# Fourteen batches' gate exponentials on ScalarE, later selections of diagonals, and a y ring of ten places

## The chip, the cores and the metric

The kernel runs on one core of a Trainium2 chip. The core has TensorE (matrix products into PSUM), VectorE, ScalarE and GpSimd (elementwise work, each with its own strengths), SyncE (here it issues transfers only), and 16 DMA engines that all queues share. The engines run their own instruction streams and wait for each other by semaphores. The metric is the device time of one execution in microseconds (us).

## What is computed

One block of a network on 16 batches of 256 tokens with 128 features, in float32: an attention-like part, then a mixture of 8 experts of which each token takes the best two. The second part, cut to what matters here:

```python
router_logits = (xhat * router_ln_w + router_ln_b) @ router_w + router_b
routing_weights, selected = jax.lax.top_k(router_logits, 2)
routing_weights = jax.nn.softmax(routing_weights, axis=-1)
h = gelu(xn_e @ w1[e] + b1[e])            # for each expert e of the token
eo = h @ w2[e] + b2[e]
combined = sum_k routing_weights[k] * eo[selected[k]]
y = _ln_stats(combined) * out_ln_w + out_ln_b
x = x + gb * y
```

With two logits a token's weights are p/(1+p) and 1/(1+p), where p = exp(second logit - first logit). These p are the gates' exponentials.

## The kernel before

The attention part runs over the 16 batches as a software pipeline of 21 iterations (`pipeline(iteration)`), each engine with its own `iteration`. Tokens are kept as 32 tiles of 128 (two a batch). During the pipeline the routing is worked out in groups of two batches (`choose`, `place`): `top` holds each token's best logits, `slot` the row of each token's copy in the DRAM buffer `xe_dram`, where rows are sorted by expert. GpSimd writes the rows there by indirect DMA (`scatter`). The last group, batches 14 and 15, comes through only after the expert tiles have begun.

The expert part then runs over 71 tiles of 128 sorted rows, `n` from 0 to 70. For one tile:

- SyncE loads the rows into one of 6 places `xg` (L322). At tile 16 it also issues the 2 MB load of `outf` (L325), the output factors.
- TensorE transposes (`turn`, L1611), multiplies by w1 (`up`, L1620, eight matmuls) and by w2 (`down`, L1630, eight matmuls). In one round it does the transpose of tile j, the up of j-2 and the down of j-3.
- VectorE, in `prepare(n)`, computes the destination rows `idxr` (L1198), scales the transposed tile (L1202) and copies the expert's w1 (L1205); then in `finish(n-3)` it adds the bias to the product and writes `y` (L1240). Between tiles 14 and 19 `prepare` also carries the table of the late tiles (`late_counts` to `late_rows`, L976 to L1001). At every even tile from 30 to 60 it adds a factor to x (L1232).
- ScalarE computes the Gelu (`hidden`, L734).
- GpSimd stores the tile's 128 rows of `y` to DRAM by indirect DMA (`store`, L482).

The places of `y` and `idxr` are a ring (`RING`, `scat`) of eight: `prepare(n)` and `finish(n)` wait until the store of tile n-8 has landed (`need_ring`). Each place has its own semaphore, `scat0` to `scat7`.

The gates: at tile 20 VectorE subtracts the two logits for all 32 token tiles (L1221, `pw`, 128x32). After the store of tile 18 GpSimd raises e to them (L487, a power on 128x32). At tile 26 VectorE makes the two weights of each token (L1224 to L1226, `gates`). From tile 28 on, at every fifth tile, GpSimd turns the weights of four token tiles into diagonal matrices (L492, `diag`, 128x1024), eight times (`DIAGONALS`).

At the end (`NG` = 8 groups of four token tiles) SyncE loads the y rows back in token order, TensorE multiplies them by the diagonals and sums (L1765), VectorE and ScalarE normalize, and the results are stored.

The order of the instructions on each engine is written out by hand; nothing schedules it.

Of the kernel before, what the change touches and what calls it, by code (L numbers as in the profile page):

```python
# [10 lines left out]
ACT = mybir.ActivationFunctionType  # L11
ALU = mybir.AluOpType
# [34 lines left out]
def build(nc, inp, out):  # L47
# [7 lines left out]
    with ExitStack() as ctx:  # L55
# [5 lines left out]
        def sem(name):  # L61
# [98 lines left out]
        LAG_U, LAG_D, LAG_S = 2, 3, 5  # L160
        RING = dict(gath=6, scat=8)
        LOADS = ((0,), (1, 2), (3, 4, 5), (6, 7))
        POOLED = NG - 2
        PARTS = [(g, 0, GROUP) for g in range(NG - 1)] + [(NG - 1, 0, 2), (NG - 1, 2, 2)]
        DIAGONALS = range(28, 28 + 5 * NG, 5)
        FACTORS = range(30, 30 + 2 * NB, 2)
# [23 lines left out]
            oT_mm sq_rdy ms_mm rsln_rdy rs_rdy t1_rdy on_rdy wob_rdy out_mm x1_rdy mv2_rdy rs2ln_rdy ve2_rdy rs2_rdy xn2_rdy xn2T_tp h2T_rdy h3_mm h3_rdy sq3_rdy rs3ln_rdy ve3_rdy rs3_rdy xrow_rdy  # L190
            set_route pad_fill pad_st endrow_rdy bt_rdy oh_rdy rank_mm slot_rdy xs_early xs_late table_rdy rb_mm rb_rdy dve_chain
            f_ld f_st f_halves f_s0 f_s pw_rdy f_fin outb_rdy
            idxr_rdy gath0 gath1 gath2 gath3 gath4 gath5 tile_tp xgT_rdy w1c_rdy up_mm hid_rdy down_mm y_rdy
            scat0 scat1 scat2 scat3 scat4 scat5 scat6 scat7
            yk_ld0 yk_ld1 yk_ld2 yk_ld3 diag_rdy acc_mm st4_rdy mv4_rdy rs4ln_rdy rs4_rdy nmr_rdy yn_rdy yo_rdy out_pool out_rdy out_st""".split()
# [60 lines left out]
        def need_tile(eng, name, j):  # L256

            if 0 <= j < NS:
                eng.wait_ge(S[name], j + 1)
# [91 lines left out]
        def _(pool):  # L351
# [48 lines left out]

            nc.gpsimd.memset(euler[:], float(np.e)).then_inc(S["f_halves"], 1)

# [73 lines left out]
            def store(n):  # L476
# [7 lines left out]
                if n == 18:  # L484
                    pool.wait_ge(S["f_halves"], 1)
                    pool.wait_ge(S["f_s0"], 1)
                    nc.gpsimd.tensor_tensor(pw[:, :, 1], euler[:], pw[:, :, 0], ALU.pow).then_inc(S["f_s"], 1)  # L487
                if n in DIAGONALS:
# [83 lines left out]
        def _(act):  # L572
# [154 lines left out]
            def hidden(n):  # L727

                if not 0 <= n < NS:
                    return  # L730
                need_tile(act, "down_mm", n - 2)
                need_tile(act, "up_mm", n)
                for c in range(NC):
                    last = nc.scalar.activation(hid[:, n % 2, c, :], up_bank[n % 2][:, c * P:(c + 1) * P], ACT.Gelu,  # L734
                                                bias=w1c[:, n % 3, FF + c:FF + c + 1])
                last.then_inc(S["hid_rdy"], 1)
                if 20 <= n < 20 + NE and n % 2 == 1:
                    put_pad(act, n - 20)
# [98 lines left out]
        def _(dve):  # L837
# [165 lines left out]
            def constants():  # L1003
# [7 lines left out]
                nc.vector.tensor_copy(bt_sb[:, :, LNW - FF], vecT[:, R_LNW:R_LNW + NE])  # L1011
                nc.vector.tensor_copy(bt_sb[:, :, LNB - FF], vecT[:, R_LNB:R_LNB + NE]).then_inc(S["bt_rdy"], 1)

# [170 lines left out]
            def prepare(n):  # L1184
# [3 lines left out]
                if n == 0:  # L1188
# [3 lines left out]
                    link(nc.vector.tensor_copy(w1s[:, :, FF:FF + NC], bt_sb[:, :, 0:NC]))  # L1192
                    chosen[n] = expert(n)
                e = chosen[n]
                need_ring(dve, "scat", n - RING["scat"])
# [24 lines left out]
                if n == 20:  # L1220
                    tt(pw[:, :, 0], top[:, :, 1], top[:, :, 0], ALU.subtract).then_inc(S["f_s0"], 1)  # L1221
                if n == 26:
                    dve.wait_ge(S["f_s"], 1)
                    link(ts(gates[:, :, 0], pw[:, :, 1], 1.0, None, ALU.add))  # L1224
# [574 lines left out]
```

## Time and profile before

| | us |
|---|---|
| median of 3 runs | 505.92 |
| lowest and highest | 505.23, 505.97 |
| the profiled execution | 503.87 |
| its span, first to last instruction | 502.1 |
| busy: TensorE (matmuls) | 438.9 |
| busy: VectorE | 397.6 |
| busy: GpSimd | 353.1 |
| busy: ScalarE | 317.2 |

The span is shorter than the execution by 1.8 us, which lie around it. The busy times are sums over stages with different limits, so no one of them tells what a step is worth: for that one has to go to the stage and see which wait ends last there. A row of the timeline reads: start, length, engine, line, operation, what it writes and reads, and in brackets the time that the engine sat idle before it and what released it. "PE" is TensorE, "PEld" its loading of weights, "DVE" VectorE, "ACT" ScalarE, "POOL" GpSimd, "SP" SyncE, a "q" behind it the engine's queue. All buffers of the expert part are parts of one tensor `work`, so `xgT`, `w1c`, `hid`, `xg` and `y` all appear as `work`; lines tell them apart.

### The profile page before, as it was taken

Reading aid. Unit: us, or ns where it says so; the run is one execution under the profiler, and the core shown is the slowest. Engines: PE = TensorE matmul, PEld = TensorE weight load, DVE = VectorE, ACT = ScalarE, POOL = GpSimd, SP = SyncE. Lnnn points to the kernel's source line nnn. Section 1 sums busy time; section 2 is a strip of 40 time slices with the busy share of each in tenths; the row PEclk is TensorE's granted clock in tenths of the full one; section 3 lists DMA queues with packets and bytes.
Section 4 is the critical chain, followed back from the end, with each engine's and each line's share of the span. In section 5 each row is a group of like instructions: output and inputs, shape, how many; then the busy total and the mean of one; then the engine's idle time right before and its main releaser. Section 6 shows DMA issues by size and latency. Waiting matters only on the chain.

```text
span 502.1 us, 11499 instructions
## 1 busy us (share of the span) xinstructions
PE 438.9 (87%) x3266; PEld 363.8 (72%) x3266; DVE 397.6 (79%) x1133; ACT 317.2 (63%) x812; POOL 353.1 (70%) x404
## 2 busy tenths in 40 slices
PE   3589999999899899889799666899789999999990
PEld 1366777776677677667667444799689999999990
DVE  2579998999989979999999965566665788776485
ACT  1166788888578578688679634675345555555575
POOL 4675875689889889899887526276468876666532
PEclk9999999999889889899999667599989999999996
DMA  6950000000000000000000141227233322226344
GB/s 157 238 148 1 7 8 7 1 17 19 25 17 22 21 23 19 21 26 13 24 23 20 47 150 34 62 70 245 64 90 80 83 86 73 69 74 212 131 134 125
DMA packets 33933, 33.66 MB, mean 67 GB/s; under 512 B 7036, under 2 KB 27680, under 8 KB 33744
## 3 DMA queue, kind: packets, MB, share of 16 engines
q1 hardware_dynamic: 27600, 22.39, 16.3%
q0 software_dynamic: 4320, 9.22, 5.5%
q10 hardware_dynamic: 1952, 1.32, 1.0%
q8 instruction: 29, 0.48, 0.4%
q14 instruction: 32, 0.26, 0.2%
HBM read 20.43 MB, written 12.48 MB: 66 GB/s over the span
## 4 chain that ended last, share of the span: by engine, by line
PE 45%; DVE 21%; POOL 19%; issue 6%; ACT 4%; DMA 2%; DVEq 1%; ACTq 1%; POOLq 0%
PE sa_ps L1620 11%; POOL xe_dram L387 6%; PE bank L1630 5%; PE sa_ps L1630 5%; PE sa_ps L1398 4%; POOL lgs L421 2%; POOL A_sb L394 2%; PE bank L1537 2%; DVE z L1046 2%; PE bank L1611 2%; PE bank L1470 2%; POOL xn L472 2%; DMA y_dram<-work,idxr 2%; PE bank L1471 2%; PE bank L1553 2%
## 5 line engine op out<-in xcount | busy, mean ns | idle before, releaser
L734 ACT ACTIVATE work<-sa_ps,work 128x128 f32<-128x128 f32 x284 | 81.2, 369 | 68.7 <-PE sa_ps L1620 68.7
L482 POOL DMA_INDIRECT y_dram<-work,idxr x71 | 72.5, 1021 | 45.4 <-DVE idxr L1198 32.0
L387 POOL DMA_INDIRECT xe_dram<-xrow,slot x64 | 72.8, 1137 | 24.1 <-issue 13.7
L1620 PE MATMUL sa_ps<-work 128*128 128x128 f32 x568 | 80.0, 285 | 0.4
L1620 PEld LDWEIGHTS sa_ps<-work 128*128 128x128 f32 x568 | 71.3, 197 | 1.4 <-issue 0.7
L1398 PE MATMUL sa_ps<-Px,wvT 64*128 64x128 f32 (+1 forms) x288 | 41.9, 341 | 3.8 <-DVE Px L1102 3.7
L1398 PEld LDWEIGHTS sa_ps<-Px,wvT 64*128 64x128 f32 x288 | 34.2, 194 | 13.8 <-DVE Px L1102 9.2
L421 POOL TENSOR_TENSOR lgs<-lgs,rsum 128x256 f32<-128x256 f32 x32 | 30.6, 974 | 16.9 <-DVE rsum L1062 16.9
L1630 PE MATMUL bank<-w2s,work 128*128 x280 | 38.2, 281 | 3.5 <-DVE work L1240 3.5
L1630 PE MATMUL sa_ps<-w2s,work 128*128 x288 | 39.0, 279 | 1.2 <-DVE work L1240 0.8
L394 POOL TENSOR_SCALAR_AFFINE_SELECT A_sb<-A_sb 128x768 f32<-128x768 f32 (+1 forms) x32 | 19.9, 647 | 26.3 <-ACT A_sb L705 26.1
L1630 PEld LDWEIGHTS bank<-w2s,work 128*128 128x128 f32 x280 | 34.8, 195 | 4.1 <-issue 4.1
L1630 PEld LDWEIGHTS sa_ps<-w2s,work 128*128 128x128 f32 x288 | 35.7, 195 | 1.8 <-issue 1.7
L1553 PE MATMUL bank<-lT,low 128*128 128x256 f32 x128 | 31.9, 392 | 0.6 <-ACT lT L693 0.6
L472 POOL TENSOR_SCALAR xn<-x_sb,mv,rs 128x128 f32<-128x128 f32 x32 | 31.8, 997 | 0.4 <-POOL rs L429 0.4
L705 ACT COPY A_sb<-sa_ps 128x1536 f32<-128x1536 f32 x16 | 23.0, 1440 | 13.2 <-PE sa_ps L1398 13.2
L1391 PE MATMUL sa_ps<-qT,kT 32*128 32x128 f32 (+1 forms) x288 | 30.9, 333 | 0.2
L1202 DVE TENSOR_SCALAR work<-bank,bt_sb 128x128 f32<-128x128 f32 x71 | 29.0, 408 | 2.4 <-issue 0.4
L1205 DVE COPY work<-work 128x516 f32 x71 | 30.7, 433 | 0.1
L1391 PEld LDWEIGHTS sa_ps<-qT,kT 32*128 32x128 f32 x288 | 24.0, 189 | 6.7 <-issue 5.6
L1198 DVE SCALAR_TENSOR_TENSOR idxr<-work,bt_sb 128x1 uint32<-128x1 f32 x71 | 21.2, 298 | 9.4 <-DMA y_dram<-work,idxr 7.7
L1553 PEld LDWEIGHTS bank<-lT,low 128*128 128x128 f32 x128 | 23.0, 189 | 5.3 <-issue 0.9
(278 smaller groups left out, 1127.7 us busy)
## 6 DMA issues: line engine op xcount, KB each, us to landing
work<-xe_dram SPq DMA_DIRECT2D x71, 69.5 KB
work<-in_w SPq DMA_DIRECT2D x1, 2048.0 KB, 9.6
outf<-outf_dram SPq DMA_DIRECT2D x1, 2048.0 KB
xrow<-y_dram SPq DMA_DIRECT2D x4, 512.0 KB, 6.2
out<-x_sb SPq DMA_DIRECT2D x7, 256.0 KB, 2.4
y_dram<-work,idxr POOLq DMA_INDIRECT x71
modb<-mod_dram SPq DMA_DIRECT2D x16, 64.0 KB, 2.8
xe_dram<-xrow,slot POOLq DMA_INDIRECT x64, 2.4
```

What stands on the lines that cost most here:

```text
L387: nc.gpsimd.indirect_dma_start(xe_dram, bass.IndirectOffsetOnAxis(slot[:, 4 * batch + column:4 * batch + column + 1], 0), xrow[:, tile, :] ...
L394: last = nc.gpsimd.affine_select(out=blocks, in_=blocks, compare_op=ALU.is_ge, fill=0.0, base=0, pattern=[[0, n] for n in blocks.shape[1:- ...
L421: last = nc.gpsimd.tensor_tensor(p, p, rsum[:, b % 2, tile * H:(tile + 1) * H].unsqueeze(2).broadcast_to([P, H, M]), ALU.mult)
L472: last = nc.gpsimd.tensor_scalar(xn[:, b % 2, tile, :], x_sb[:, 2 * b + tile, :], mv1[:, b % 4, tile, 0:1], rs1[:, b % 4, tile:tile + 1], ...
L482: nc.gpsimd.indirect_dma_start(y_dram, bass.IndirectOffsetOnAxis(idxr[:, n % RING["scat"]:n % RING["scat"] + 1], 0), y[:, n % RING["scat"] ...
L734: last = nc.scalar.activation(hid[:, n % 2, c, :], up_bank[n % 2][:, c * P:(c + 1) * P], ACT.Gelu, bias=w1c[:, n % 3, FF + c:FF + c + 1])
L1205: nc.vector.tensor_copy(w1c[:, n % 3], w1s[:, bass.ds(e, 1), :].squeeze(1)).then_inc(S["w1c_rdy"], 1)
L1391: return mm(o, kT[d, b % 2, s * P:(s + 1) * P], qT[d, b % 2, t], start=True, stop=True)
L1398: return mm(o, wvT[m, b % 4, h // 2, s * P:(s + 1) * P], Px[m, b % 2, h // 2, t], start=True, stop=True)
L1553: last = mm((b4, b5)[n // 2][:, (n % 2) * T:(n % 2 + 1) * T], low2[:, n, :], lT[:, b % 2, :], start=True, stop=True)
L1620: last = mm(up_bank[n % 2][:, c * P:(c + 1) * P], w1c[:, n % 3, c * P:(c + 1) * P], xgT[:, n % 3, :], start=True, stop=True)
L1630: last = mm(down_bank[n % 2][:, 0:D], hid[:, n % 2, c, :], w2s[:, bass.ds(chosen[n], 1), c, :].squeeze(1), start=c == 0, stop=c == NC - 1)
```

## The change

The ring of y rows and index rows gets ten places instead of eight, with two more semaphores. The subtraction is done in two parts: token tiles 0 to 27 (batches 0 to 13, `AHEAD` = 28) at the start of tile 0, the last four at tile 20 as before. ScalarE computes the exponentials of the first 28 with its Exp before its first Gelu; GpSimd's power is left with the last 4. The diagonals are made at tiles 36, 40, ... 64 instead of 28, 33, ... 63. The semaphore `f_halves` is replaced by a third count of `set_route`, and an increment that nobody waited for (`bt_rdy`) is gone.

```diff
@@
-        RING = dict(gath=6, scat=8)
+        RING = dict(gath=6, scat=10)
...
-        DIAGONALS = range(28, 28 + 5 * NG, 5)
+        DIAGONALS = range(36, 36 + 4 * NG, 4)
+        AHEAD = 2 * (NB - 2)
@@ GpSimd
-            nc.gpsimd.memset(euler[:], float(np.e)).then_inc(S["f_halves"], 1)
+            nc.gpsimd.memset(euler[:], float(np.e)).then_inc(S["set_route"], 1)
...
                 if n == 18:
-                    pool.wait_ge(S["f_halves"], 1)
-                    pool.wait_ge(S["f_s0"], 1)
-                    nc.gpsimd.tensor_tensor(pw[:, :, 1], euler[:], pw[:, :, 0], ALU.pow).then_inc(S["f_s"], 1)
+                    pool.wait_ge(S["set_route"], 3)
+                    pool.wait_ge(S["f_s0"], 2)
+                    nc.gpsimd.tensor_tensor(pw[:, AHEAD:NT, 1], euler[:, AHEAD:NT], pw[:, AHEAD:NT, 0], ALU.pow).then_inc(S["f_s"], 1)
@@ ScalarE, hidden(n)
+                if n == 0:
+                    act.wait_ge(S["f_s0"], 1)
+                    nc.scalar.activation(pw[:, 0:AHEAD, 1], pw[:, 0:AHEAD, 0], ACT.Exp).then_inc(S["f_s"], 1)
                 need_tile(act, "down_mm", n - 2)
@@ VectorE, constants()
-                nc.vector.tensor_copy(bt_sb[:, :, LNB - FF], vecT[:, R_LNB:R_LNB + NE]).then_inc(S["bt_rdy"], 1)
+                nc.vector.tensor_copy(bt_sb[:, :, LNB - FF], vecT[:, R_LNB:R_LNB + NE])
@@ VectorE, prepare(n), n == 0
                     chosen[n] = expert(n)
+                    tt(pw[:, 0:AHEAD, 0], top[:, 0:AHEAD, 1], top[:, 0:AHEAD, 0], ALU.subtract).then_inc(S["f_s0"], 1)
@@ VectorE, prepare(n)
                 if n == 20:
-                    tt(pw[:, :, 0], top[:, :, 1], top[:, :, 0], ALU.subtract).then_inc(S["f_s0"], 1)
+                    tt(pw[:, AHEAD:NT, 0], top[:, AHEAD:NT, 1], top[:, AHEAD:NT, 0], ALU.subtract).then_inc(S["f_s0"], 1)
                 if n == 26:
-                    dve.wait_ge(S["f_s"], 1)
+                    dve.wait_ge(S["f_s"], 2)
```

How it stands on the engines, in rows that give line, operation, what is written and read, and the semaphores waited for. The line numbers of the changed kernel are up to 5 higher. First VectorE at tile 0, before and then after:

```order
625 L1192 COPY work<-bt_sb 128x8x4 [waits ld_w1,ld_b2]
626 L1182 TENSOR_LOAD exp_i [waits table_rdy,dve_chain]
627 L1182 ISA x2
628 L1198 ISA [waits gath0]
629 L1198 SCALAR_TENSOR_TENSOR idxr<-work,bt_sb 128x1
```

```order
625 L1196 COPY work<-bt_sb 128x8x4 [waits ld_w1,ld_b2]
626 L1186 TENSOR_LOAD exp_i [waits table_rdy,dve_chain]
627 L1186 ISA x2
628 L1198 TENSOR_TENSOR pw<-top 128x28
629 L1203 ISA [waits gath0]
630 L1203 SCALAR_TENSOR_TENSOR idxr<-work,bt_sb 128x1
```

The subtraction on 28 columns stands between the load of the expert's number and the index row. On ScalarE at the same place, before and then after:

```order
421 L760 ACTIVATE ln<-ss,eps_col 128x2
422 L762 ACTIVATE rs<-ln 128x2
423 L765 ACTIVATE xrow<-h,rs 128x136 x2
424 L734 ACT_TABLE_LOAD
425 L734 ACTIVATE work<-sa_ps,work 128x128 x16
```

```order
421 L764 ACTIVATE ln<-ss,eps_col 128x2
422 L766 ACTIVATE rs<-ln 128x2
423 L769 ACTIVATE xrow<-h,rs 128x136 x2
424 L734 ACTIVATE pw<-pw 128x28
425 L738 ACT_TABLE_LOAD
426 L738 ACTIVATE work<-sa_ps,work 128x128 x16
```

The exponential comes behind the last rows of batch 14 and ahead of the table load for the Gelu. VectorE at tile 14, before and then after, behind the finish of tile 10:

```order
786 L1240 TENSOR_TENSOR work<-sa_ps,bt_sb 128x128
787 L1198 ISA [waits gath2,scat6]
788 L1198 SCALAR_TENSOR_TENSOR idxr<-work,bt_sb 128x1
789 L1202 ISA [waits tile_tp,up_mm]
790 L1202 TENSOR_SCALAR work<-bank,bt_sb 128x128
791 L1205 ISA [waits hid_rdy]
792 L1205 COPY work<-work 128x516
793 L978 TENSOR_SCALAR early_i<-early_i 1x8
```

```order
787 L1245 TENSOR_TENSOR work<-sa_ps,bt_sb 128x128
788 L1203 ISA [waits gath2,scat4]
789 L1203 SCALAR_TENSOR_TENSOR idxr<-work,bt_sb 128x1
790 L1207 ISA [waits tile_tp,up_mm]
791 L1207 TENSOR_SCALAR work<-bank,bt_sb 128x128
792 L1210 ISA [waits hid_rdy]
793 L1210 COPY work<-work 128x516
794 L982 TENSOR_SCALAR early_i<-early_i 1x8
```

The index row of tile 14 waited for place 6, the store of tile 6; it now waits for place 4, the store of tile 4. The rows of the table behind it (line 978, now 982) stand where they stood. On GpSimd, from the stores of tiles 24 and 25 on, before and then after:

```order
319 L482 DMA y_dram<-work,idxr 12288x128 [waits y_rdy,idxr_rdy] x2
320 L387 DMA xe_dram<-xrow,slot 66560x139
321 L482 DMA y_dram<-work,idxr 12288x128 [waits y_rdy,idxr_rdy] x3
322 L492 AFFINE_SELECT diag<-gates 128x1024 [waits pw_rdy]
323 L482 DMA y_dram<-work,idxr 12288x128 [waits y_rdy,idxr_rdy] x5
324 L492 AFFINE_SELECT diag<-gates 128x1024
325 L482 DMA y_dram<-work,idxr 12288x128 [waits y_rdy,idxr_rdy] x5
```

```order
319 L483 DMA y_dram<-work,idxr 12288x128 [waits y_rdy,idxr_rdy] x2
320 L388 DMA xe_dram<-xrow,slot 66560x139
321 L483 DMA y_dram<-work,idxr 12288x128 [waits y_rdy,idxr_rdy] x11
322 L493 AFFINE_SELECT diag<-gates 128x1024 [waits pw_rdy]
323 L483 DMA y_dram<-work,idxr 12288x128 [waits y_rdy,idxr_rdy] x4
324 L493 AFFINE_SELECT diag<-gates 128x1024
325 L483 DMA y_dram<-work,idxr 12288x128 [waits y_rdy,idxr_rdy] x4
```

The first selection moves behind the store of tile 36, and four stores stand between two selections where five stood. SyncE's, TensorE's and the other rows keep their order.

## Rows read from the trace of the kernel before

**Rows 1.** Busy time by stage: window, each engine's busy us (instructions), clock, DMA share.

```profile
440.00:460.00 20.00, 19.96 (x173) 19.46 (x172) 14.14 (x44) 11.54 (x41) 12.74 (x13) 1.00 0.32 84
```

**Rows 2.** Chain that ended last, in order of time: start us, length us, what.

```profile
342.26 8.01 DMA y_dram<-work,idxr
...
366.29 2.00 PE bank L1630 x8
...
371.08 0.89 PE sa_ps L1620 x8
...
385.00 0.97 PE sa_ps L1620 x8
...
412.11 0.95 PE sa_ps L1620 x8
...
467.99 0.95 PE sa_ps L1620 x8
```

**Rows 3.** Timeline of VectorE: start, length, instruction, idle before it and its releaser.

```profile
318.58 0.22 DVE L1198 SCALAR_TENSOR_TENSOR idxr<-work,bt_sb 128x1 uint32<-128x1 f32 x1 [1.09 <-issue]
...
346.06 0.29 DVE L1240 TENSOR_TENSOR work<-bank,bt_sb 128x128 f32<-128x128 f32 x1 [0.24 <-issue]
...
347.56 0.29 DVE L1240 TENSOR_TENSOR work<-sa_ps,bt_sb 128x128 f32<-128x128 f32 x1 [0.24 <-issue]
350.43 0.22 DVE L1198 SCALAR_TENSOR_TENSOR idxr<-work,bt_sb 128x1 uint32<-128x1 f32 x1 [2.58 <-DMA y_dram<-work,idxr]
...
365.86 0.29 DVE L1240 TENSOR_TENSOR work<-bank,bt_sb 128x128 f32<-128x128 f32 x1 [1.21 <-issue]
...
386.11 0.22 DVE L1198 SCALAR_TENSOR_TENSOR idxr<-work,bt_sb 128x1 uint32<-128x1 f32 x1 [1.31 <-DMA y_dram<-work,idxr]
...
405.36 1.73 DVE L1198 SCALAR_TENSOR_TENSOR idxr<-work,bt_sb 128x1 uint32<-128x1 f32 x1
...
408.00 0.28 DVE L1240 TENSOR_TENSOR work<-bank,bt_sb 128x128 f32<-128x128 f32 x1
...
408.99 0.28 DVE L1240 TENSOR_TENSOR work<-sa_ps,bt_sb 128x128 f32<-128x128 f32 x1
```

**Rows 4.** Timeline of SyncE's queue, the load of outf.

```profile
342.25 0.44 SPq L325 DMA_DIRECT2D outf<-outf_dram  x1
```

**Rows 5.** Busy time, single microseconds: PE, PEld, DVE, ACT, POOL, clock, DMA, GB/s.

```profile
347.00:348.00 1.00, 1.00 (x12) 1.00 (x11) 0.60 (x2) 0.49 (x2) 1.00 (x1) 1.00 1.12 442
...
367.00:368.00 1.00, 1.00 (x7) 1.00 (x6) 0.42 (x3) 0.00 (x0) 0.94 (x1) 0.50 0.30 71
```

**Rows 6.** Timeline of TensorE, table stretch.

```profile
354.56 0.30 PE L1611 MATMUL bank<-ident,work 128*128 128x128 f32 x1
...
366.29 2.00 PE L1630 MATMUL bank<-w2s,work 128*128 x8 [1.62 <-DVE work L1240]
```

**Rows 7.** Timeline of GpSimd: a store, the power, a selection.

```profile
339.59 0.96 POOL L482 DMA_INDIRECT y_dram<-work,idxr  x1 [0.33 <-issue]
...
374.62 5.47 POOL L487 TENSOR_TENSOR pw<-euler,pw 128x32 f32<-128x32 f32 x1
...
405.95 1.11 POOL L492 TENSOR_SCALAR_AFFINE_SELECT diag<-gates 128x1024 f32<-128x1024 f32 x1
```

**Rows 8.** Line 1198, what its idle time waited for: us in total, times.

```profile
  DMA y_dram<-work,idxr: 7.7, 7
```

**Rows 9.** Durations ns min/median/max of the powers (lines 429, 487) and the subtraction.

```profile
L429 POOL TENSOR_TENSOR rs<-ve,halves x16: 722/724/1077, 13.7 to 232.7; 128x2 f32<-128x2 f32 x16
...
L1221 DVE TENSOR_TENSOR pw<-top x1: 219/219/219, 369.4 to 369.4; 128x32 f32<-128x32 f32 x1
L487 POOL TENSOR_TENSOR pw<-euler,pw x1: 5467/5467/5467, 374.6 to 374.6; 128x32 f32<-128x32 f32 x1
```

**Rows 10.** Timeline of ScalarE at the start of the tiles.

```profile
321.71 1.14 ACT L734 ACTIVATE work<-sa_ps,work 128x128 f32<-128x128 f32 x4 [1.08 <-PE sa_ps L1620]
```

More of the change, by code:

```diff
@@ L190, in build @@
             oT_mm sq_rdy ms_mm rsln_rdy rs_rdy t1_rdy on_rdy wob_rdy out_mm x1_rdy mv2_rdy rs2ln_rdy ve2_rdy rs2_rdy xn2_rdy xn2T_tp h2T_rdy h3_mm h3_rdy sq3_rdy rs3ln_rdy ve3_rdy rs3_rdy xrow_rdy
-            set_route pad_fill pad_st endrow_rdy bt_rdy oh_rdy rank_mm slot_rdy xs_early xs_late table_rdy rb_mm rb_rdy dve_chain
-            f_ld f_st f_halves f_s0 f_s pw_rdy f_fin outb_rdy
+            set_route pad_fill pad_st endrow_rdy oh_rdy rank_mm slot_rdy xs_early xs_late table_rdy rb_mm rb_rdy dve_chain
+            f_ld f_st f_s0 f_s pw_rdy f_fin outb_rdy
             idxr_rdy gath0 gath1 gath2 gath3 gath4 gath5 tile_tp xgT_rdy w1c_rdy up_mm hid_rdy down_mm y_rdy
-            scat0 scat1 scat2 scat3 scat4 scat5 scat6 scat7
+            scat0 scat1 scat2 scat3 scat4 scat5 scat6 scat7 scat8 scat9
             yk_ld0 yk_ld1 yk_ld2 yk_ld3 diag_rdy acc_mm st4_rdy mv4_rdy rs4ln_rdy rs4_rdy nmr_rdy yn_rdy yo_rdy out_pool out_rdy out_st""".split()
```

## The prediction

> **What bounds the kernel now.** The change touches only the second half of the program, so I read from there. The chain of work that ended last, followed in order of time, comes first; the reader is to see in it which engine each stretch belongs to. From about 318 us the expert tiles run, 71 of them. In the steady part TensorE is never without work: it is busy 19.96 of 20 us [rows 1], and the chain holds nothing but its matmuls: the up matmuls of 28 tiles start between 412.11 and 467.99 us, 1.996 us a tile [rows 2]. No saving on VectorE, ScalarE or GpSimd can shorten that part. What can be had lies where TensorE waits.
>
> There are two such places. The first hangs on the ring of y rows. The chain has a piece of 8.01 us that is a transfer: the store of tile 6, issued at 342.26 us, lands at about 350.3 [rows 2]. VectorE's row of index 14 (tile 14 wants tile 6's place in the ring of eight) stands idle for 2.58 us until it lands [rows 3]. The store is slow since SyncE had issued the 2 MB load of outf at 342.25 [rows 4]; in the microsecond from 347 the queues move 442 GB/s [rows 5]. From there VectorE is the bound: it has the late table to work out (tiles 14 to 19) and goes from the finish of tile 10 at 347.56 to that of tile 15 at 365.86 [rows 3], 18.30 us for five tiles, of which 2.58 are the wait and 15.72 work, 3.1 us a tile against TensorE's 2.0. TensorE waits for VectorE in this stretch, last for 1.62 us before 366.29 [rows 6], and is the bound from then on.
>
> The second place is GpSimd's power on 128x32 elements, 5.47 us at 374.62 [rows 7]. No store goes out meanwhile. Stores after it are late, and VectorE waits for them again, for instance 1.31 us before 386.11 [rows 3]. In all VectorE's index rows wait seven times and 7.7 us for stores [rows 8]; 2.58 is the first, 5.1 are the six after the power. TensorE feels little of those 5.1: its up matmuls start at 371.08 and 385.00, seven tiles later (1.989 us each), and then at 412.11, thirteen tiles later (2.085 each) [rows 2]. Against 1.996 that is 1.16 us lost in thirteen tiles.
>
> **The change part by part.**
>
> *Ring of ten.* Tile 14 now needs the store of tile 4, tile 15 that of tile 5, issued at 339.59 [rows 7], before the big load. The store of tile 6 is wanted by tile 16 only, whose index row comes two tiles of 3.1 us behind the one of tile 14: started at 347.8 instead of 350.43 that is about 354, after the landing at 350.3. So the 2.58 us wait goes whole, and since VectorE bounds the next five tiles, what follows moves up by the same 2.58, if TensorE can keep up: it needs 10 us for five tiles where VectorE needs 15.7. Its end is at the point at which TensorE takes over. Lower bound 1.0 (a next wait, below), upper 2.58; I take **-2.58**, since every step behind it is VectorE's own.
>
> *The power on 128x4, the rest an exponential on ScalarE.* The trace has no power on 4 columns. On 2 columns it takes 724 ns, on 32 it takes 5467 [rows 9]: 158 ns a column, so 1.04 us for 4. GpSimd gets 4.4 us back just where its stores were late, the ring gives two tiles (4 us) of tolerance beside it, and the first selections leave the stretch. So all six waits should go. Worth: at most the 1.16 us that TensorE lost over its usual pace, at least about 0.3 (part of that loss may be something else, as the matmuls there show no wait of their own). I take **-0.7**, the middle.
>
> *The subtraction in two parts.* The larger one (128x28) now stands at the start of the tiles, ahead of the index row of tile 0, which starts at 318.58 [rows 3]. The old one on 32 columns takes 219 ns [rows 9]. Behind it on VectorE all work of tile 0 is queued, and TensorE and GpSimd wait for that. Between 0 (under the register load ahead of it) and 0.22; I take **+0.2**. The remainder at tile 20 is shorter than before and off the path.
>
> *The exponential.* The four activations of tile 0's hidden part, 128 columns each, take 1.14 us [rows 10], so one on 28 columns takes at most 0.29. ScalarE waits for the subtraction, which is done by about 318.8, while ScalarE is at earlier work and the table load; queued behind the exponential is tile 0's hidden part, before which ScalarE sat idle 1.08 us, until 321.71 [rows 10]. Cost 0; without that cover 0.3. The order shows it ahead of the table load, so no table load is added.
>
> *Selections of diagonals every fourth tile from 36.* Eight as before, 1.11 us each. They are wanted when the tiles are over, after 468 [rows 2]; the last now comes behind the store of tile 64, one tile later than before, six stores ahead of the end. Cost 0. The extra semaphores and the removed increments: nothing.
>
> **A rule to weigh.** While GpSimd ran the selection at 405.95 [rows 7], VectorE's index row took 1.73 us instead of 0.22 [rows 3]. The Trainium skill (SBUF — State Buffer, Who interferes with whom) says that GpSimd and a VectorE instruction that needs the shared pair of ports shut each other out for a whole instruction. By that rule, which the row agrees with, a selection costs VectorE up to its own length wherever it stands, so moving eight of them is worth nothing by itself; what counts is whether VectorE has room, which is the slower rival below.
>
> **The sum.** -2.58 - 0.7 + 0.2 = -3.1 us. The profiled execution took 503.87 us (span 502.1, 1.8 around it), so 500.8 for its like. The median of the runs is 505.92, 2.05 above; I carry the same difference over: **502.8 us**.
>
> **The rivals.**
>
> *The clock.* After the wait of 1.62 us TensorE's granted clock stood at 0.50 in the microsecond from 367, where it is 1.00 in the one from 347 [rows 5]: 1.2 instead of 2.4 GHz. The eight matmuls at 366.29 took 2.00 us against 0.89 later, and from them to the up matmuls at 371.08 [rows 2] it took 4.79 us for what goes in about 2.9 (a tile and a half at 1.996): 1.9 lost. By my timetable TensorE waits at the same place, about 2 us, so I expect one fall, as now. If none comes, another 1.9 goes: 500.9. If it falls twice, or falls in the middle of the table stretch and stays low, 1.9 comes back: 504.7. The shape of the waits speaks for one fall; that their places shift by 2.6 us leaves both others open.
>
> *A new wait takes the old one's place.* The tile loads issued behind outf on SyncE's queue may be late. The transpose of tile 17 ran at 354.56 without an idle time recorded before it [rows 6]; it would now be wanted at about 353.1. If its load was only just there, the start moves by at most 1.5 us and then TensorE still has room, since VectorE reaches tile 17 three tiles of 3.1 us after 347.8, at about 357. The Trainium skill (DMA: Bandwidth & Descriptors, Queues, rings and completion order) says that descriptors of one queue are taken in ring order, so these loads would indeed stand behind the big one; no row here times one of them. Were the whole 2.58 eaten up in some such way, -0.7 + 0.2 = -0.5 would be left: 505.4.
>
> *The change doesn't do it:* the waits move from index rows to the finishes and nothing is gained: 505.9. Against it: seven waits, all at the ring.
>
> *Slower: VectorE has no room for the selections.* Every selection now stands four tiles from the next and always with an even tile, to which a factor addition belongs. Take VectorE's tile at 1.50 us (the finishes at 346.06 and 347.56, with all issue gaps [rows 3]), two additions of 0.43 and 1.5 us shut out (1.73 - 0.22): 8.4 us for four tiles, against TensorE's 7.98. That is 0.4 us lost in each of eight groups, all of the 3.1 gained. At a tile of 1.55 us it is 8.57, 0.59 us in each group, 4.7 in all: 505.92 - 3.1 + 4.7 = 507.5. Slower by over 0.2% begins at a tile of 1.53. Against it: with the five-tile spacing of now the same count gives 10.1 us (5 times 1.50, 2.5 times 0.43, 1.5) for TensorE's 9.98, and yet TensorE held its 1.996; and when VectorE was behind, it finished tiles at 408.00 and 408.99 [rows 3], 1.0 us apart, as its issue gaps close up; with 1.0 the four tiles take 6.4.
>
> **How the numbers follow.** Forecast 502.8 (502.1 to 503.7 by the bounds of its terms): 0.55. No fall of the clock, 500.9: 0.10. A second fall, 504.7: 0.12. A new wait, 505.4: 0.11. Nothing, 505.9: 0.04. VectorE without room, 507.5: 0.08. A measurement can tell about 0.2%, 1.0 us. Faster than 504.9: 0.55 + 0.10 + 0.12 = 0.77; the same: 0.15; slower: 0.08. The range takes in the forecast, both cases of the clock and the new wait: 500.8 to 505.4; outside it stand 0.12 and what lies beyond the edges of the clock's cases.
>
> **What would show it.** In the profile of the changed kernel no index row should wait for a store. VectorE's finish of tile 15 should come about 2.4 us earlier (2.58 less 0.2), near 363.5, and the next matmuls with it. The power should take about 1.0 us, and TensorE keep 2.0 us a tile from there to the end. The granted clock after 363 us tells the first rival. If the chain still runs through a transfer of y rows near 345 us, or TensorE waits for VectorE at tiles 36 to 64, I am wrong.

## The result, and the profile after

| | before | after |
|---|---|---|
| median, us | 506.09 | 500.47 |
| lowest to highest, us | 503.10 to 509.25 | 499.11 to 504.73 |
| the profiled execution, us | 503.87 | 499.39 |
| its span, us | 502.1 | 497.6 |

Each has 11 runs. The ratio of the changed kernel to the one before is 0.9905, with a 95% interval from 0.9878 to 0.9931: 4.8 us faster, between 3.5 and 6.2. The forecast was 3.1 us faster, and 502.8 us; measured are 500.47. It is faster, as forecast, by more than forecast. The range was 500.8 to 505.4: the median is 0.3 us under it, and by the ratio, on the 505.92 us from which the forecast was made, it is 501.1, just inside. The measured time is near that of the rival in which the clock does not fall (500.9); why I take that for chance is told below.

To see where it went I cut the second half of the program at VectorE's finishes of tiles 10, 15, 20 and 70. A cut at a finish has a trap, which shows below: a selection on GpSimd can hold a single finish back, so the long stretch is not cut in the middle. All in us, from the one profiled execution of each kernel, the experiments' too (the experiments are told further down):

| | start of finish 10 | 10 to 15 | 15 to 20 | 20 to 70 | 70 to the end | span |
|---|---|---|---|---|---|---|
| before | 347.56 | 18.30 | 9.26 | 100.25 | 26.7 | 502.1 |
| after | 347.24 | 15.88 | 8.28 | 99.11 | 27.1 | 497.6 |
| ring of ten alone | 347.69 | 15.64 | 8.63 | 99.03 | 26.9 | 497.9 |
| exponential alone | 349.78 | 18.68 | 8.28 | 99.19 | 26.8 | 502.7 |
| after, again | 347.03 | 15.85 | 8.27 | 99.09 | 27.1 | 497.3 |
| ring of nine alone | 349.37 | 16.04 | 8.27 | 99.51 | 27.1 | 500.3 |
| after, old places of the selections | 349.80 | 16.00 | 8.27 | 99.29 | 27.0 | 500.4 |
| before, outf load at tile 22 | 347.96 | 15.89 | 8.27 | 101.02 | 26.8 | 499.9 |
| after, register load earlier | 350.09 | 13.46 | 8.01 | 99.23 | 27.1 | 497.9 |
| the same and the table in eight pieces | 350.37 | 9.05 | 10.16 | 99.07 | 27.2 | 495.8 |

From before to after the span lost 4.5 us: 0.3 ahead of finish 10, 2.4 in the table stretch (10 to 15), 1.0 behind it, 1.1 over the fifty tiles to 70; the last part grew by 0.4. That growth is no accident of one profile: the part behind tile 70 took 26.7 to 26.8 us in the three kernels with a ring of eight places, and 26.9 to 27.2 in all with nine or ten. The sum had no term for it, and no run shows its cause.

First the waits. The view of one line, the index rows' (1203, before 1198), gives what the idle time before its instructions waited for: what, us in total, times. For after:

```profile
L1203 DVE SCALAR_TENSOR_TENSOR idxr<-work,bt_sb x71: 203/219/1051, 318.8 to 463.5; 128x1 uint32<-128x1 f32 x71
its engine sat idle before it (us, times) until:
  issue: 0.3, 1
```

The 7.7 us in seven waits of [rows 8] are gone, all of them. VectorE's timeline of after, the rows that answer to [rows 3]:

```profile
318.62 0.21 DVE L1198 TENSOR_TENSOR pw<-top 128x28 f32<-128x28 f32 x1 [0.96 <-DVE work L1196]
318.80 0.22 DVE L1203 SCALAR_TENSOR_TENSOR idxr<-work,bt_sb 128x1 uint32<-128x1 f32 x1
...
347.24 0.29 DVE L1245 TENSOR_TENSOR work<-sa_ps,bt_sb 128x128 f32<-128x128 f32 x1 [0.36 <-PE sa_ps L1635]
347.48 0.22 DVE L1203 SCALAR_TENSOR_TENSOR idxr<-work,bt_sb 128x1 uint32<-128x1 f32 x1
...
350.14 0.29 DVE L1245 TENSOR_TENSOR work<-bank,bt_sb 128x128 f32<-128x128 f32 x1 [0.86 <-DVE ending L986]
...
363.12 0.29 DVE L1245 TENSOR_TENSOR work<-bank,bt_sb 128x128 f32<-128x128 f32 x1 [1.21 <-issue]
```

The index row of tile 14 starts at 347.48 right behind the finish of tile 10, where it had stood idle for 2.58 us until 350.43 [rows 3]. The finish of tile 15 came at 363.12 (before 365.86). The new subtraction stands ahead of tile 0's index row, which starts 0.22 us later.

The chain that ended last, of after, where the 8.01 us transfer of [rows 2] had been:

```profile
348.02 0.89 PE bank L1635 x8
...
351.96 0.91 PE bank L1635 x8
352.90 0.06 DVE work L1245
...
354.76 1.04 DVE exp_f L972
...
360.88 1.04 DVE row_f L978
361.95 0.30 DVEq L1186
362.25 0.04 issue
362.29 0.19 DVEq L1186
...
363.55 1.15 PE bank L1635 x8
...
365.08 0.95 PE sa_ps L1625 x8
366.03 0.94 PE sa_ps L1635 x8
...
367.31 0.95 PE sa_ps L1625 x8
368.26 0.89 PE bank L1635 x8
...
371.23 0.95 PE sa_ps L1625 x8
```

No transfer is left in it, though the store of tile 6 is as slow as before. The transfers issued in the window from 342 to 343 us, with the time to landing, in us, last:

```profile
y_dram<-work,idxr POOLq DMA_INDIRECT x1, 8.4
```

Nobody waits for it any more. In the chain TensorE comes first, to 352.9, VectorE's table from there to 363.4, TensorE again from 363.55 on. The pieces on the queue at line 1186 are the load of the next expert's number into registers; they stand in the open behind each piece of the table, and the last two experiments move them.

TensorE's own timeline of after, and the window that answers to the clock of [rows 5]:

```profile
363.55 1.15 PE L1635 MATMUL bank<-w2s,work 128*128 x8 [1.63 <-DVE work L1245]
```

```profile
366.00:367.00 1.00, 0.98 (x9) 0.81 (x9) 0.92 (x4) 0.87 (x4) 0.69 (x2) 1.00 0.23 67
```

The wait for VectorE is as long as before (1.63 against 1.62 us [rows 6]), and yet the granted clock stays at 1.00, which is 2.4 GHz; before, it had gone to 0.50 [rows 5]. The eight matmuls took 1.15 instead of 2.00 us.

GpSimd's and ScalarE's timelines of after:

```profile
372.01 1.04 POOL L488 TENSOR_TENSOR pw<-euler,pw 128x4 f32<-128x4 f32 x1
373.25 1.03 POOL L483 DMA_INDIRECT y_dram<-work,idxr  x1 [0.20 <-issue]
```

```profile
319.41 0.21 ACT L734 ACTIVATE pw<-pw 128x28 f32<-128x28 f32 x1
319.64 1.28 ACT L738 ACT_TABLE_LOAD   x1
321.92 1.14 ACT L738 ACTIVATE work<-sa_ps,work 128x128 f32<-128x128 f32 x4 [1.00 <-PE sa_ps L1625]
```

The power takes 1.04 us instead of 5.47, and the next store goes out 1.2 us behind its start. The exponential takes 0.21 us, and ScalarE still sits idle for 1.00 us behind the table load, waiting for TensorE (1.08 before [rows 10]): it is covered.

### The profile page after: what moved, and what is told of

Read it like the earlier page. It is cut to its first block, busy times and chain, and to the rows that moved or that the text cites. A ratio compares the mean times of both kernels' runs of the same rounds, so it can differ in the third digit from the quotient of the medians.

```text
span 497.6 us, 11499 instructions
## 1 busy us (share of the span) xinstructions
PE 436.6 (88%) x3266; PEld 363.0 (73%) x3266; DVE 398.8 (80%) x1134; ACT 316.9 (64%) x813; POOL 347.0 (70%) x404
## 4 chain that ended last, share of the span: by engine, by line
PE 49%; POOL 23%; DVE 16%; issue 6%; ACT 4%; DVEq 1%; DMA 0%; ACTq 0%; POOLq 0%
PE sa_ps L1625 12%; POOL xe_dram L388 8%; PE sa_ps L1635 6%; PE bank L1635 6%; PE sa_ps L1403 3%; POOL lgs L422 3%; POOL A_sb L395 3%; PE bank L1616 2%; POOL xn L473 2%; PE bank L1475 2%; POOL kT L445 2%; PE sa_ps L1396 2%; PE bank L1476 2%; PE bank L1600 2%; PE bank L1542 2%
## 5 line engine op out<-in xcount | busy, mean ns | idle before, releaser
L1072 DVE TENSOR_TENSOR_SCAN z<-ones,wvT 128x256 f32<-128x256 f32 x32 | 26.2, 860 | 0.1
```

## The experiments

Eight kernels ran, in two batches of four, each batch on one chip together with the kernel before. The medians of before there were 503.50 us (20 runs) and 505.11 us (21 runs). Ratios are to before of the same batch.

### The ring of ten alone

```diff
-        RING = dict(gath=6, scat=8)
+        RING = dict(gath=6, scat=10)
```

With it go the two semaphores `scat8` and `scat9`; to make room for them `bt_rdy` is left out and `f_halves` is counted in `set_route`, as in the changed kernel. The power stays on 128x32, no exponential is on ScalarE, and the selections stand where they stood.

> The ring of ten alone: the power on GpSimd stays at 128x32 (5.47 us) and the selections stay at every fifth tile from 28. Theory A (the ring is what matters, it hides the late stores too): no index row waits for a store, the finish of tile 15 comes 2.6 us earlier than before, and the time is 3 to 5 us below the kernel before, like the whole change. Theory B (the two parts add up, the ring takes only the wait at tile 14 and the exponential is needed for the rest): about 2.6 us below before, and a wait for stores of 0.5 us or more remains after the power. Rival (the gain is mostly in the power): less than 1.5 us below.

Measured: 499.65 us (9 runs), ratio 0.9912 [0.9883, 0.9941]: the ring alone gives what the whole change gives. VectorE's index row of tile 14 follows the finish at once, and no index row waits for a store, though the long power is still there. Timelines of VectorE and GpSimd, and the list of what line 1198 waited for:

```profile
347.69 0.29 DVE L1240 TENSOR_TENSOR work<-sa_ps,bt_sb 128x128 f32<-128x128 f32 x1 [0.33 <-PE sa_ps L1630]
347.93 0.22 DVE L1198 SCALAR_TENSOR_TENSOR idxr<-work,bt_sb 128x1 uint32<-128x1 f32 x1
```

```profile
372.55 5.47 POOL L487 TENSOR_TENSOR pw<-euler,pw 128x32 f32<-128x32 f32 x1
378.21 1.03 POOL L482 DMA_INDIRECT y_dram<-work,idxr  x1 [0.19 <-issue]
```

```profile
  issue: 1.7, 3
```

The stretch from 20 to 70 took 99.03 us, as in after (99.11). So two more places absorb a power of 5.47 us by themselves. Expected were 3 to 5 us if the ring is what matters and about 2.6 if the two parts added up; measured are 4.4.

This kernel also shows the trap of the cut. From 20 to 40 it took 40.50 us, from 40 to 70 58.53, against 40.03 and 59.08 of after. I first took that for an effect of the selections. It is one row: the index row ahead of the finish of tile 40 was held up by a selection. VectorE's timeline of this kernel:

```profile
410.06 1.82 DVE L1198 SCALAR_TENSOR_TENSOR idxr<-work,bt_sb 128x1 uint32<-128x1 f32 x1
...
412.46 0.28 DVE L1240 TENSOR_TENSOR work<-sa_ps,bt_sb 128x128 f32<-128x128 f32 x1
```

GpSimd's selection ran at 410.75 for 1.11 us. TensorE's matmuls around it kept their pace, so only the mark moved, and no time.

### The exponential alone

```diff
+        AHEAD = 2 * (NB - 2)
...
-                    nc.gpsimd.tensor_tensor(pw[:, :, 1], euler[:], pw[:, :, 0], ALU.pow).then_inc(S["f_s"], 1)
+                    nc.gpsimd.tensor_tensor(pw[:, AHEAD:NT, 1], euler[:, AHEAD:NT], pw[:, AHEAD:NT, 0], ALU.pow).then_inc(S["f_s"], 1)
...
+                if n == 0:
+                    act.wait_ge(S["f_s0"], 1)
+                    nc.scalar.activation(pw[:, 0:AHEAD, 1], pw[:, 0:AHEAD, 0], ACT.Exp).then_inc(S["f_s"], 1)
```

and the subtraction in two parts. The ring stays at eight, the selections where they stood.

> The exponentials of fourteen batches on ScalarE alone: ring of eight, selections at every fifth tile from 28. Theory A and B: the 2.6 us wait of tile 14 for the store of tile 6 stays, the six later waits (5.1 us) shrink to under 1.5 us; TensorE regains at most 0.7 to 1.2 us and loses 0.2 at the start: 0.3 to 1.0 us below before. Rival (the gain is mostly in the power): 3 us or more below before.

Measured: 502.86 us (12 runs), ratio 0.998 [0.9957, 1.0004], 1.0 us with an interval that touches no change. The timeline of VectorE at tile 14, and the list of line 1203's waits:

```profile
353.02 0.22 DVE L1203 SCALAR_TENSOR_TENSOR idxr<-work,bt_sb 128x1 uint32<-128x1 f32 x1 [2.95 <-DMA y_dram<-work,idxr]
```

```profile
  DMA y_dram<-work,idxr: 3.3, 2
```

The wait at tile 14 is there (10 to 15 took 18.68 us), and of the six behind the power one of 0.36 us is left. From 20 to 70 it took 99.19 us, 1.1 less than before. The 1.1 us is therefore what the late stores behind the power cost in the profile of before, and either part of the change gets it: the two are alternatives, not terms of a sum. In the changed kernel, with ten places, the shorter power has nothing left to save.

### The changed kernel again

```diff
(no edit: the changed kernel as it is, beside the others of the batch)
```

> The changed kernel as it is, once more, beside the parts on one chip, for the spread of its times against the granted clock. If its larger gain (4.8 instead of 3.1 us) is the clock not falling after the table tiles, executions divide by mean clock: those at 0.936 or more lie some 2 to 4 us below those at 0.930 or less, and the profile shows the clock at 1.00 or at 0.50 behind the finish of tile 15. If the larger gain comes from elsewhere, time and mean clock go separate ways.

Measured: 499.66 us (6 runs), ratio 0.9922 [0.9896, 0.9949]. It agrees with the first measurement and cannot be told from the ring alone. Of the 17 executions of the changed kernel, the eleven with a mean granted clock of 0.936 or 0.937 took 499.05 to 501.69 us, the three at 0.930 or less 500.82, 503.12 and 504.73: time goes with the mean clock, as the first expectation had it. But that does not make the gain: in this batch the mean clock was 0.938 over the twenty executions of before and 0.935 over the six of after, and the profiled executions of before (with the fall) and of after (without it) both have 0.936.

### A ring of nine alone

```diff
-        RING = dict(gath=6, scat=8)
+        RING = dict(gath=6, scat=9)
```

with `scat8` in the place of `bt_rdy`.

> A ring of nine alone. Tile 14 then needs the store of tile 5 (issued at 339.59 us before the big load) and tile 15 that of tile 6, which lands at about 350.3; tile 15's index row would come at about 350.4. Theory A: nine places take nearly the whole wait, at most 0.3 us is left at tile 15, and the time is within 1 us of the ring of ten (2.5 to 4.5 us below before); the waits after the power go too. Rival (ten are needed): a wait of 1 us or more remains at tile 15 or 16, and half of the gain is missing.

Measured: 499.14 us (6 runs), ratio 0.9892 [0.9856, 0.9928]. Line 1198's waits in its profile:

```profile
  DMA y_dram<-work,idxr: 4.5, 4
```

The expectation that the waits behind the power would go too was wrong. None of the four is in the table stretch (16.04 us from 10 to 15, as with ten). They are at tiles 29, 31, 33 and 36, behind the power, and cost at most 0.4 us from 20 to 70 (99.51 against 99.1). One place more is enough for the big wait; the tenth takes the waits behind the power, and its worth is below what these runs can tell.

### The old places of the selections

In the changed kernel:

```diff
-        DIAGONALS = range(36, 36 + 4 * NG, 4)
+        DIAGONALS = range(28, 28 + 5 * NG, 5)
```

> The changed kernel with the selections of diagonals back at tiles 28, 33, ... 63; ring of ten and exponentials on ScalarE stay. Two theories on why the stretch from the finish of tile 40 to that of tile 70 takes 59.1 us in the changed kernel but 58.5 with the ring of ten alone. If every selection costs TensorE a little wherever it stands (it shuts VectorE out), fewer stand behind tile 40 here (five instead of seven) and this stretch takes 58.5 to 58.7 again, while the one from 20 to 40 (40.0) grows by as much: no difference in all, within 0.3 us. If a selection costs more together with a factor addition at an even tile, the whole is 0.5 us or more below the changed kernel. Rival of the forecast (VectorE without room every fourth tile): 1 us or more below.

Measured: 500.29 us (10 runs), ratio 0.9914 [0.9883, 0.9946]; 20 to 70 took 99.29 us, 0.2 more than after. (The theory by which 40 to 70 would go back to 58.5 us was wrong: it took 59.28; the 58.5 was the moved mark.) The place of the selections makes no difference that can be measured. VectorE has the room for them at either spacing, which answers the slower rival. The Trainium skill (SBUF — State Buffer, Who interferes with whom) says that GpSimd and a VectorE instruction on the shared ports exclude each other. The index row of 1.82 us above agrees, as the one of 1.73 did [rows 3]. In after eight index rows take 0.88 to 1.05 us instead of 0.22, one for each selection; that TensorE is never without work there, and that moving the selections changes nothing, shows that it costs no time while VectorE isn't the bound.

### The load of outf six tiles later

In the kernel before, with its ring of eight:

```diff
-                if j == 16:
+                if j == 22:
```

> The kernel before, ring of eight, with one edit: the 2 MB load of outf is issued ahead of tile 23's load (j == 22) instead of tile 17's. If that load is what makes the store of tile 6 take 8 us, the index row of tile 14 no longer waits (under 0.3 us) and the finish of tile 15 comes 2 to 2.6 us earlier; the waits after the power stay. In all 2 to 3 us below before, unless the load now slows a store that is wanted (tiles 20 to 24 are three us apart, so a slow store has four tiles or 12 us). Rival (the store is slow for another reason, such as GpSimd's own lateness): the wait at tile 14 stays at 2 us or more and nothing is gained.

This asks why the store of tile 6 took 8.01 us. Measured: 501.77 us (10 runs), ratio 0.9941 [0.9909, 0.9973]. VectorE's timeline at tile 14, its list of waits, and TensorE's two waits, which VectorE's rows of tiles 27 and 28 end:

```profile
347.96 0.29 DVE L1240 TENSOR_TENSOR work<-sa_ps,bt_sb 128x128 f32<-128x128 f32 x1 [0.24 <-issue]
348.20 0.22 DVE L1198 SCALAR_TENSOR_TENSOR idxr<-work,bt_sb 128x1 uint32<-128x1 f32 x1
```

```profile
  DMA y_dram<-work,idxr: 5.7, 5
```

```profile
382.31 1.13 PE L1620 MATMUL sa_ps<-work 128*128 128x128 f32 x8 [0.41 <-DVE work L1205]
385.12 0.33 PE L1611 MATMUL bank<-ident,work 128*128 128x128 f32 x1 [0.79 <-DVE work L1202]
```

With a ring of eight and no load beside it, tile 14 does not wait, and the table stretch takes 15.89 us. The traces' semaphore events give the stores themselves, from issue to the last landing: those of tiles 6 and 8 took 8.0 and 6.2 us in before and 2.5 and 2.3 here, while here those of tiles 12 and 14, issued beside the moved load and while it was still under way, took 7.3 and 5.0. The load was the cause of the slow store, and the ring only shelters VectorE from it.

What stays are waits behind the power, five of 5.7 us in all (six of 5.1 in before), since the ring still has eight places; that is why it gains less than the ring of ten. They are not the moved load's doing: it was issued at 354.70 and took 10.2 us, so it had landed at 364.9, ahead of the power. Its row in the list of the transfers issued from 354 to 355 us (size, us to landing), then VectorE's finish of tile 20, then GpSimd's power:

```profile
outf<-outf_dram SPq DMA_DIRECT2D x1, 2048.0 KB, 10.2
```

```profile
372.12 0.29 DVE L1240 TENSOR_TENSOR work<-sa_ps,bt_sb 128x128 f32<-128x128 f32 x1 [0.24 <-issue]
```

```profile
372.72 5.47 POOL L487 TENSOR_TENSOR pw<-euler,pw 128x32 f32<-128x32 f32 x1
```

TensorE now feels the waits (0.41 and 0.79 us where it had no recorded wait), and 20 to 70 took 101.02 us, 0.8 more than before. The last two rows say where the 0.8 can come from: the power starts 0.6 us behind that finish here, as in the rings of nine and ten, but 0.5 ahead of it in before (374.62 [rows 7] against the finish below), where TensorE's lower clock had held the tiles up while GpSimd went on. Relative to the tiles the stores are 1.1 us later here. VectorE's timeline of before:

```profile
375.12 0.29 DVE L1240 TENSOR_TENSOR work<-sa_ps,bt_sb 128x128 f32<-128x128 f32 x1 [0.65 <-PE sa_ps L1630]
```

### The register load ahead of the table

In the changed kernel, `prepare(n)` loads the next tile's expert before it works on the table:

```diff
+                if n + 1 < NS:
+                    chosen[n + 1] = expert(n + 1)
                 if n == 14:
...
-                if n + 1 < NS:
-                    chosen[n + 1] = expert(n + 1)
```

> The changed kernel with the load of the next expert's number moved ahead of the late table's instructions in tiles 14 to 19; nothing else. My reading of what bounds the changed kernel there: VectorE, 15.9 us from the finish of tile 10 to that of tile 15, with 0.85 us idle after each of the table's pieces for the register load. If that is so, about 0.6 us goes in each of five tiles: the stretch takes 12.5 to 13.5 us and the time falls 2 to 3.5 us below the changed kernel. If TensorE or a transfer is the bound as soon as VectorE moves, less than 1 us is gained.

Measured: 498.32 us (6 runs), ratio 0.9861 [0.9819, 0.9903]. In the same batch the changed kernel with the old places of the selections had 500.29 us; the two intervals still overlap a little, so it is the stretch that shows the gain. VectorE's timeline:

```profile
352.24 0.15 DVE L986 CAST ending<-count_i 1x8 f32<-1x8 int32 x1
352.54 0.29 DVE L1245 TENSOR_TENSOR work<-bank,bt_sb 128x128 f32<-128x128 f32 x1
```

In after VectorE stood idle for 0.86 us between the same instruction and this finish; here nothing is recorded. From 10 to 15 it took 13.46 us instead of 15.88. This says what bounds the table stretch, once the store is out of the way, beside the table's own work: the load of the next expert's number into registers, which had stood in the open between the table's last instruction and the finish.

### The table in eight pieces

On top of that the late table is worked out in eight pieces at tiles 11, 13, 15, 17, 19, 21, 23 and 25 instead of six at 14 to 19, and the selections stand at their old places:

```diff
-                if n == 14:
+                if n == 11:
                     late_counts()
-                if n == 15:
+                if n == 13:
...
-                if n == 16:
-                    tile_bins(NS - NA, 2 * NE)
+                if n == 15:
+                    past_bins(NS - NA, 2 * NE)
+                if n == 17:
+                    sum_bins(NS - NA, 2 * NE)
```

and in the same way for the rest (`tile_bins` and `tile_rows` are each cut between their subtraction and their sum).

> The edit of the load, and the late table cut into eight pieces at tiles 11, 13, ... 25 instead of six at 14 to 19, and the selections at every fifth tile from 28. If VectorE's table is all that keeps TensorE from its 2.0 us a tile, the stretch from the finish of tile 10 to that of tile 20 takes 20 to 21 us instead of 24.1 and the time is 3 to 4.5 us below the changed kernel. If a single piece of 1.0 us and its register load still makes TensorE wait, about 2 us. A rival (TensorE's clock or the loads behind outf bound the stretch): under 1 us.

Measured: 496.99 us (6 runs), ratio 0.9839 [0.9799, 0.9880]. It is the fastest of all, 8.1 us under before by the ratio, and 3.3 us by the medians under the changed kernel with the old places of the selections in the same batch, with intervals that do not touch. From the kernel with the earlier register load it cannot be told by its ratio (the intervals overlap; 1.3 us by the medians). The stretch from 10 to 20 took 19.2 against 21.5 us, but here the cut misleads: `prepare(11)` and `prepare(13)` come ahead of the finish of tile 10, so two of the eight pieces lie outside of it. From tile 0's index row to the finish of tile 10 this kernel took 30.0 us where the other took 28.7. From the index row to the finish of tile 70 it took 148.2 against 149.4: the pieces are worth 1.2 us, not 2.3. That is enough to hide the table: no wait of TensorE is recorded from 340 us to the end of the fifty tiles. Busy time by stretch of this kernel (window, its length, then the busy us of PE, PEld, DVE, ACT and POOL, the clock, the DMA share, GB/s), and then of after:

```profile
347.00:372.00 25.00, 24.81 (x211) 23.95 (x211) 21.23 (x66) 13.69 (x48) 18.88 (x19) 1.00 0.55 171
```

```profile
347.00:372.00 25.00, 22.00 (x180) 20.77 (x179) 17.91 (x61) 11.78 (x42) 15.31 (x15) 1.00 0.43 129
```

TensorE is busy 24.81 of 25 us there, against 22.00 (and 23.73 with the earlier register load alone).

## Why the prediction was right, and where it was off

**The ring: right.** The term was -2.58 us, from VectorE's wait. The table stretch got 2.42 shorter, the finish of tile 15 came at 363.12 where 363.5 was forecast, and the ring alone reproduces it. The reading behind it, that the whole wait would go since VectorE is the bound in these tiles and the next store wanted had landed, held in every kernel with nine or ten places.

**The power and the exponential: the amount was mis-sized, and it was booked to the wrong part.** I took -0.7, the middle of 0.3 and 1.16. The fifty tiles from 20 gave 1.14, the upper bound; and that bound was itself too low for an execution without the fall of the clock, where the runs point to 1.9 (see the sum below). The power itself came out at 1.04 us as worked out from two widths. What the prediction did not say is that the ring would have done this alone: the step "two tiles of tolerance beside it" held the whole answer, and a sum by parts hid it. The ring alone gives 99.03 us there, the exponential alone 99.19, both together 99.11.

**The subtraction and the exponential on ScalarE: right.** The index row of tile 0 is 0.22 us later (+0.2 forecast), ScalarE's exponential is covered. In the profile of after the 0.22 is lost again by tile 10, which finishes 0.3 us earlier than before; that stretch differs between executions by more (below).

**The selections: right.** Cost 0 as forecast; at the old places the time is the same. The slower rival, that VectorE would have no room, did not happen. Busy time of after in the window of the later tiles, in the same columns:

```profile
400.00:468.00 68.00, 68.00 (x585) 66.73 (x584) 50.23 (x144) 39.04 (x137) 43.66 (x42) 1.00 0.35 110
```

TensorE is never without work there.

**The clock: the step that failed, beside the size of the late stores.** I expected one fall behind the table stretch "as now", a term of zero, since TensorE would wait at the same place. It waits at the same place, 1.63 us, and the clock did not fall. The rival's mechanism happened, but its price was wrong as well. I had put 4.79 us against 2.9 from the steady pace (a tile and a half at 1.996 is 2.99). After has the same instructions from 363.55 to 367.31, 3.76 us, at a clock of 1.00, and again from 368.26 to 371.23, 2.97 us. So the steady price was right, but 0.8 of the 1.9 is the start behind a wait, which is slow at the full clock too (the first eight matmuls take 1.15 us, the later ones 0.89), and the fall costs the other 1.0. 15 to 20 went from 9.26 to 8.28 us, the same 1.0.

It is also not the change that prevents the fall. The kernels with the exponential alone, the old places of the selections and nine places have waits of TensorE of 1.63, 1.61 and 1.62 us behind the table and 8.27 or 8.28 us from 15 to 20, and the exponential alone still has the big wait at tile 14. It is the closest to before: behind that wait its TensorE waits 0.61, 0.28, 1.28 and 1.63 us for VectorE's finishes, before 0.61, 0.28, 1.28 and 1.62. TensorE's timeline of it, and the window behind:

```profile
368.89 1.15 PE L1635 MATMUL bank<-w2s,work 128*128 x8 [1.63 <-DVE work L1245]
```

```profile
369.00:370.00 1.00, 1.00 (x8) 0.85 (x8) 0.96 (x4) 0.00 (x0) 0.49 (x1) 1.00 0.00 0
```

Of the ten profiles only that of before shows the fall. So the 1.0 us is a difference between executions, as far as ten profiles tell; in how many executions of before it comes can't be seen, since only one is profiled.

**The new wait, and nothing gained: did not happen.** The loads behind outf were in time; the transposes never became the bound. They do stand behind the big load, though: with outf at tile 22 the tile load issued behind it at 358.04 took 7.2 us to land, at 365.2, where others took 2.2 to 3.3.

**The sum.** The profiles differ by 4.5 us. It looks as if 1.0 of it were the fall, so that 3.5 would be left without it; four kernels taken together speak against that. From finish 10 to finish 70 (the sum of three columns of the table):

| | late stores behind the power | none |
|---|---|---|
| wait at tile 14 | 127.8 (before, with the fall) | 126.2 (exponential alone) |
| no wait at tile 14 | 125.2 (before, outf load at tile 22) | 123.3 (after) |

In the three without a fall the late stores cost 1.9 us (125.2 less 123.3) and the wait 2.9 (it is 2.95 us long in the exponential alone, 2.58 in before). With 1.9 and 2.6 on top of 123.3 before should take 127.8 without any fall, and it took 127.8 with one: the 1.0 us that the fall cost behind the table came back behind the power, since GpSimd's stores gained on the tiles meanwhile. So the term that was too small is the late stores: I measured TensorE's loss of 1.16 in an execution in which the fall hid some 0.8 of it, and then went halfway to 0.3. With 1.9 in place of 0.7 the sum is -4.3. The two measurements gave 4.8 [3.5, 6.2] and 3.9 [2.6, 5.2] us, which it fits well; the forecast of 3.1 fits the second and is under the first. This rests on one profile of each kernel (the five with nine or ten places and the table as it was took 123.2 to 123.8), and a profile of before without the fall, which would test it, was not taken. That the number came out near the rival without a fall I take for chance: its 1.9 was wrong twice over, in the price and in its place.

The range of the forecast was too narrow by its own terms: 503.7 leaves out the ring's lower bound of 1.0, with which the upper edge would be 504.8.

## What to carry to other kernels

When a ring of buffers shows waits at two places with different causes, ask of each remedy what it does alone: here two more places cured both, and the dearer edit beside them bought nothing that could be measured. A wait for a slow store has two cures, more places or moving the big load out of its way; the second cures only the wait that the load made, and here left the one behind the power. A loss read off a profile can be too small when something else had delayed the same tiles just ahead of it. When the wait is gone, follow the chain again: the next 2.4 us were a register load behind VectorE's own work, which one moved line removed, and spreading the side work over more tiles gave some 1.2 us more. When work is moved across a mark, a stretch cut at that mark no longer compares.

## What the runs showed of the hardware

**One and the same wait lowers the clock in one execution and not in others.** TensorE waited 1.61 to 1.63 us behind the table in before, after and four experiments; the granted clock went to 0.50 (1.2 GHz) in before only. One of the four, the exponential alone, has the same four waits in a row as before and did not fall. A fall can't be forecast from the length of the wait.

**Executions differ in when the clock comes back as the tiles begin.** In all ten profiles it is at 0.50 around 316 us, where the attention part ends and TensorE is busy 3.0 to 4.2 of the 6 us from 312 to 318. The windows from 324 to 328, of after and then of the kernel with the earlier register load:

```profile
324.00:328.00 4.00, 4.00 (x34) 4.00 (x33) 3.47 (x15) 2.27 (x8) 2.84 (x4) 0.88 0.47 91
```

```profile
324.00:328.00 4.00, 4.00 (x21) 4.00 (x20) 2.79 (x11) 1.89 (x7) 2.80 (x3) 0.50 0.32 75
```

In five profiles (before, after and after again, the ring of ten, the later outf load) this window has 0.81 to 0.90, tile 0's index row starts at 318.5 to 319.2 and tile 10 is finished at 347.0 to 348.0. In the other five it has 0.50 to 0.64, the index row comes at 320.4 to 321.4 and the finish at 349.4 to 350.4. That is 2 us between executions of programs that are the same up to there but for the subtraction, the exponential, the places of the ring and, in the kernel with eight pieces, two pieces of the table; as much as most terms of the sum. So spans of single profiles are not to be compared; stretches behind finish 10 are. With the same table and nine or ten places, 10 to 15 took 15.64 to 16.04 us in five profiles and 10 to 70 123.2 to 123.8, so a difference under half a us says nothing.

**A store of 128 rows took 8.01 us beside the 2 MB load** [rows 2]; with the load moved the same store took 2.5 us, and the store that now stood beside the load took 7.3. In before I had seen the two only together; the moved load showed that it is the cause.
